# The last tile's output in a half and two quarters, its first LoRA half behind the mix of tile 14, and the gather index on VectorE

## The reference

```
x = x + einsum('bct,bcd->bdt', x, W0[cond])
base = einsum('bti,oi->bto', x, W) + b
lora = einsum('btr,bro->bto', einsum('bti,bir->btr', x, A[adapter]), B[adapter])
return x + base + lora * 2
```

## Time and profile before

| | |
|---|---|
| median of the runs (lowest, highest) | 85.22 us (85.20, 85.53) |
| the profiled execution | 85.35 us, of which its span is 83.6 us |
| busy: PE, DVE, ACT, POOL | 79.6, 59.3, 52.0, 35.0 us |
| granted clock of TensorE | full (1.0, the level of 2.4 GHz) in all slices |
| chain that ended last | PE 85%, DMA 6%, ACT's queue 3%, ACT 2%, issue 1%, DVE 1% |
| stores of 256 KB, of 128 KB (the last two) | 2.4 us, 1.7 us from issue to landing |

### The profile page before, as it was taken

How to read it: one execution, slowest core, us unless ns; L and a number is a source line. 1 busy time by engine, 2 the same in 40 slices (tenths; PEclk the granted TensorE clock), 3 DMA queues, 4 the chain that set the end, 5 groups by cost and what they waited for, 6 DMA issues and landing times.

```text
span 83.6 us, 1999 instructions
## 1 busy us (share of the span) xinstructions
PE 79.6 (95%) x521; PEld 71.8 (86%) x521; DVE 59.3 (71%) x154; ACT 52.0 (62%) x179; POOL 35.0 (42%) x75
## 2 busy tenths in 40 slices
PE   4999999999999999999999999999999999999970
PEld 2368688999899999999999999999999999999930
DVE  2048495885888787777878787888787777876540
ACT  1545757766566675958666666666685957669120
POOL 6128888844442617080715344342617080303000
PEclk9999999999999999999999999999999999999999
DMA  0999779899776768676586878676874734120333
GB/s 13 307 347 315 143 199 261 165 365 329 209 239 163 239 196 245 197 206 213 143 250 171 238 178 241 174 248 151 219 211 159 177 110 152 45 92 7 119 125 125
DMA packets 15997, 16.06 MB, mean 192 GB/s; under 512 B 10225, under 2 KB 10482, under 8 KB 15986
## 3 DMA queue, kind: packets, MB, share of 16 engines
q1 hardware_dynamic: 14016, 11.74, 47.4%
q0 software_dynamic: 1248, 4.06, 17.0%
q10 hardware_dynamic: 722, 0.14, 0.9%
HBM read 11.74 MB, written 4.19 MB: 191 GB/s over the span
## 4 chain that ended last, share of the span: by engine, by line
PE 85%; DMA 6%; ACTq 3%; ACT 2%; issue 1%; DVE 1%
PE z_ps L548 58%; PE z_ps L585 9%; DMA a_raw<-in_lora_a 6%; PE y_ps L596 4%; PE y_ps L600 4%; PE y_ps L598 4%; PE ht_ps L572 2%; ACTq L323 1%; PE z_ps L580 1%; PE ht_ps L626 1%; ACT L317 1%; PE y_last L608 1%; PE y_ps L608 1%; ACTq L313 1%; DVE y_sb L534 1%
## 5 line engine op out<-in xcount | busy, mean ns | idle before, releaser
L548 PE MATMUL z_ps<-wa,x_hi 128*128 128x288 f32 (+2 forms) x240 | 50.3, 301 | 0.0
L548 PEld LDWEIGHTS z_ps<-wa,x_hi 128*128 128x128 f32 x240 | 38.0, 188 | 1.8 <-issue 0.5
L548 PE MATMUL z_ps<-wa,x_lo 128*128 128x288 f32 (+2 forms) x120 | 35.5, 296 | 0.0
L548 PEld LDWEIGHTS z_ps<-wa,x_lo 128*128 128x128 f32 x120 | 22.6, 188 | 0.0
L291 POOL DMA_INDIRECT b_raw<-in_lora_b,b_index_slot x16 | 17.6, 1097 | 4.4 <-POOL b_index_slot L289 4.4
L300 POOL CAST m_hi<-m_raw 128x128 fp32r<-128x128 f32 x15 | 4.4, 293 | 31.5 <-ACT m_raw L337 31.5
L480 DVE TENSOR_TENSOR z_lo<-z_ps,z_hi 128x256 fp32r<-128x256 f32 x30 | 11.3, 420 | 6.4 <-ACT z_hi L381 6.4
L381 ACT CAST z_hi<-z_ps 128x256 fp32r<-128x256 f32 x30 | 9.7, 376 | 9.7 <-PE z_ps L585 9.6
L337 ACT COPY m_raw<-w_raw 32x32 f32 x64 | 13.8, 216 | 1.8 <-DVE w_raw L502 1.2
L439 DVE TENSOR_TENSOR x_lo<-x_raw,x_hi 128x512 fp32r<-128x512 f32 x14 | 9.7, 690 | 3.5 <-ACT x_hi L349 3.5
L460 DVE TENSOR_TENSOR b_lo<-b_raw,b_hi 128x512 fp32r<-128x512 f32 x15 | 10.4, 693 | 1.6 <-ACT b_hi L369 1.1
(11 more groups left out here) (51 smaller groups left out, 78.8 us busy)
## 6 DMA issues: line engine op xcount, KB each, us to landing
out<-y_sb SPq DMA_DIRECT2D x15, 256.0 KB, 2.4
x_raw<-in_xt SPq DMA_DIRECT2D x14, 256.0 KB, 2.9
a_raw<-in_lora_a SPq DMA_DIRECT2D x60, 32.0 KB
first_sb<-in_first SPq DMA_DIRECT2D x2, 384.0 KB, 4.0
first_sb<-in_first SPq DMA_DIRECT2D x3, 256.0 KB, 4.8
b_raw<-in_lora_b,b_index_slot POOLq DMA_INDIRECT x16, 4.0
bias_sb<-in_bias SPq DMA_DIRECT2D x1, 256.0 KB, 5.2
out<-y_sb SPq DMA_DIRECT2D x2, 128.0 KB, 1.7
```

The lines of the kernel that those rows point to most:

```text
L548: done = nc.tensor.matmul(target, (x_lo if lo_x else x_hi)[s][:, k, :], moving(lo_w), start=first and not lo_x and not lo_w, stop=last and ...
```

## The change

- GpSimd no longer makes `b_index`; VectorE does (`index_b`), behind its second `add_identity` and ahead of the first `rest_w`.
- TensorE's list for the last tiles: `transpose_h(14)` moves ahead of `mix(13)`, `lora(14)` behind that mix and ahead of chunks 2 and 3 of tile 15's half 0; `last_chunk(2, 1)` moves behind `mix(14)` and `lora(15, 0)`.
- Half 0 of tile 15 is mixed like other tiles, in three split matmuls of 256 columns (`mix_last_half`), half 1 in two fp32 matmuls of 128 columns (`mix_last_quarter`), the last one into the `ht_ps` bank. ScalarE rounds half 0 and copies half 1 in quarters; VectorE makes the rest of half 0; GpSimd splits M of tile 15 too.
- Bias adds and stores go by half, quarter, quarter; the last store is issued from ScalarE's queue.
- On ScalarE `round_h(15)` and `build_m(15)` move behind `round_z(14)`; on VectorE `mask_ht(14)` moves ahead of `rest_b(15)`, and `rest_h(15)` behind `rest_z(14)`.

```diff
+    PARTS = (slice(0, HALF), slice(HALF, HALF + P), slice(HALF + P, O))
...
+        def y_part(n):
+            return (y_ps[LAST % 2][:, 0:HALF], y_last[:, 0:P], ht_ps[:, 0:P])[n]
...
-            pool.wait_ge(ids_p_loaded, 16)
-            pool.tensor_copy(r_of_p[:, :], ids_p_sb[:, TILES:TILES + 1]).then_inc(r_ready, 1)
-            pool.wait_ge(r_ready, 1)
-            pool.tensor_scalar(b_index[:, :], ids_p_sb[:, 0:TILES], float(R), r_of_p[:, 0:1],
-                               ALU.mult, ALU.add).then_inc(b_index_ready, 1)
...
-            for u in range(LAST):
+            for u in range(TILES):
                 split_m(u)
...
-            build_m(LAST)
-            round_h(LAST)
             for half in range(2):
                 round_z(LAST - 1, half)
-            for half in range(2):
-                act.wait_ge(lora_done, 2 * LAST + half + 1)
-                act.copy(z_sb[:, cols(half)], z_of(LAST, half)).then_inc(z_copied, 1)
+            round_h(LAST)
+            build_m(LAST)
+            round_z(LAST, 0)
+            act.wait_ge(lora_done, 2 * LAST + 2)
+            for n in range(2):
+                act.copy(z_sb[:, n * P:(n + 1) * P], z_of(LAST, 1)[:, n * P:(n + 1) * P]).then_inc(z_copied, 1)
+            act.wait_ge(y_ready, LAST + len(PARTS))
+            act.dma_start(out_rows[LAST * P:(LAST + 1) * P, PARTS[-1]],
+                          y_sb[LAST % 2][:, PARTS[-1]]).then_inc(last_part_stored, 16)
...
+            add_identity(1)
+            index_b()
+            rest_w(0)
+            for k in range(1, KC - 1):
...
             rest_h(LAST - 1)
+            mask_ht(LAST - 1)
             rest_b(LAST)
-            mask_ht(LAST - 1)
             finish_y(LAST - 2)
-            rest_h(LAST)
             rest_z(LAST - 1, 0)
             rest_z(LAST - 1, 1)
+            rest_h(LAST)
             mask_ht(LAST)
             finish_y(LAST - 1)
+            rest_z(LAST, 0)
...
+            def mix_last_half():
+                pe.wait_ge(z_hi_ready, 2 * LAST + 1)
+                pe.wait_ge(m_ready, LAST + 1)
+                pe.wait_ge(y_ready, LAST - 1)
...
+            def mix_last_quarter(n):
+                pe.wait_ge(z_copied, n + 1)
...
-            mix_last(0)
-            mix_last(1)
+            mix_last_half()
+            mix_last_quarter(0)
+            mix_last_quarter(1)
```

More of the change, by code:

```diff
@@ L98, in lora_residual_program @@
         z_lo = [sb(f"z_lo{s}", [P, O], F32R) for s in range(2)]
-        z_sb = sb("z_sb", [P, O], F32)
+        z_sb = sb("z_sb", [P, HALF], F32)
         y_sb = [sb(f"y_sb{s}", [P, O], F32) for s in range(2)]
@@ L116, in lora_residual_program @@
         y_stored = [sem(f"y_stored{s}") for s in range(2)]
+        last_part_stored = sem("last_part_stored")
         zeros_ready = sem("zeros_ready")
@@ L250, in _ @@
             store_y(LAST - 1)
-            for half in range(2):
-                sp.wait_ge(y_ready, LAST + 1 + half)
-                sp.dma_start(out_rows[LAST * P:(LAST + 1) * P, cols(half)],
-                             y_sb[LAST % 2][:, cols(half)]).then_inc(y_stored[LAST % 2], 16)
+            for n, at in enumerate(PARTS[:-1]):
+                sp.wait_ge(y_ready, LAST + 1 + n)
+                sp.dma_start(out_rows[LAST * P:(LAST + 1) * P, at],
+                             y_sb[LAST % 2][:, at]).then_inc(y_stored[LAST % 2], 16)
             sp.wait_ge(y_stored[0], 16 * (TILES // 2))
             sp.wait_ge(y_stored[1], 16 * (TILES // 2 + 1))
+            sp.wait_ge(last_part_stored, 16)
         @block.gpsimd
@@ L488, in finish_y, with index_b @@
                                         ALU.add).then_inc(y_ready, 1)
+            def index_b():
+                dve.wait_ge(ids_p_loaded, 16)
+                nc.vector.tensor_copy(r_of_p[:, :], ids_p_sb[:, TILES:TILES + 1]).then_inc(r_ready, 1)
+                dve.wait_ge(r_ready, 1)
+                nc.vector.tensor_scalar(b_index[:, :], ids_p_sb[:, 0:TILES], float(R), r_of_p[:, 0:1],
+                                        ALU.mult, ALU.add).then_inc(b_index_ready, 1)
             dve.wait_ge(ident_ready, 1)
             add_identity(0)
-            for k in range(KC - 1):
+            add_identity(1)
+            index_b()
+            rest_w(0)
+            for k in range(1, KC - 1):
                 add_identity(k + 1)
@@ L522, in _ @@
             rest_h(LAST - 1)
+            mask_ht(LAST - 1)
             rest_b(LAST)
-            mask_ht(LAST - 1)
             finish_y(LAST - 2)
-            rest_h(LAST)
             rest_z(LAST - 1, 0)
             rest_z(LAST - 1, 1)
+            rest_h(LAST)
             mask_ht(LAST)
             finish_y(LAST - 1)
+            rest_z(LAST, 0)
             dve.wait_ge(y_stored[LAST % 2], 16 * (LAST // 2))
[L532 to L535, removed]
+            for n, at in enumerate(PARTS):
+                dve.wait_ge(y_computed, LAST + 1 + n)
+                nc.vector.tensor_tensor(y_sb[LAST % 2][:, at], y_part(n), bias_sb[:, at], ALU.add).then_inc(y_ready, 1)
         @block.tensor
@@ L601, in mix @@
                                  skip_group_check=True).then_inc(y_computed, 1)
[L603 to L609, removed]
+            def mix_last_half():
+                s = LAST % 2
+                pe.wait_ge(z_hi_ready, 2 * LAST + 1)
+                pe.wait_ge(m_ready, LAST + 1)
+                pe.wait_ge(y_ready, LAST - 1)
+                nc.tensor.matmul(y_part(0), m_hi[s][:, :], z_hi[s][:, cols(0)], start=True, stop=False,
+                                 skip_group_check=True)
+                nc.tensor.matmul(y_part(0), m_lo[s][:, :], z_hi[s][:, cols(0)], start=False, stop=False,
+                                 skip_group_check=True)
+                pe.wait_ge(z_ready, 2 * LAST + 1)
+                nc.tensor.matmul(y_part(0), m_hi[s][:, :], z_lo[s][:, cols(0)], start=False, stop=True,
                                  skip_group_check=True).then_inc(y_computed, 1)
+            def mix_last_quarter(n):
+                pe.wait_ge(z_copied, n + 1)
+                nc.tensor.matmul(y_part(1 + n), m_raw[LAST % 2][:, :], z_sb[:, n * P:(n + 1) * P], start=True,
+                                 stop=True, skip_group_check=True).then_inc(y_computed, 1)
             def first_chunk(k):
@@ L654, in _ @@
             last_chunk(1, 0)
+            transpose_h(LAST - 1)
             mix(LAST - 2)
-            transpose_h(LAST - 1)
+            lora(LAST - 1, 0)
+            lora(LAST - 1, 1)
             last_chunk(2, 0)
             last_chunk(3, 0).then_inc(main_done, 1)
-            lora(LAST - 1, 0)
-            lora(LAST - 1, 1)
             last_chunk(0, 1)
@@ L663, in _ @@
             transpose_h(LAST)
-            last_chunk(2, 1)
             mix(LAST - 1)
             lora(LAST, 0)
+            last_chunk(2, 1)
             last_chunk(3, 1)
             lora(LAST, 1)
-            mix_last(0)
-            mix_last(1)
+            mix_last_half()
+            mix_last_quarter(0)
+            mix_last_quarter(1)
 def kernel(**inputs):
```

## The result

The changed kernel takes 84.68 us (median of five, 84.62 to 84.87) against 85.40 for the kernel before on the same chip (85.20 to 85.53): ratio 0.9925, 95% interval 0.9902 to 0.9948. The forecast was 84.7 against 85.22. The profiled execution has a span of 83.0 us instead of 83.6.

What follows compares the result with a forecast made beforehand. TensorE, busy 79.6 of 83.6 us, bounds the kernel; only stalls, start and end can shorten it. Gains 0.06 + 0.14 + 0 + 0.22 + 0.13 = 0.55 us take the median from 85.22 to 84.7, range 84.35 to 85.3.

Steps and rivals of the forecast that it cites:

- Index earlier: At the start, `b_index` made on VectorE stands 1.3 us earlier, gathers 0 to 2 go out about 1.2 us sooner.
- The stall before tile 0's LoRA: TensorE's loads idle 0.26 us before tile 0's LoRA matmuls, waiting for gather 0; a stall of some 0.2 goes.
- The cap: Tile 2's first matmul needs `z_lo` of tile 0, so the earlier gather gains 0.06 us there, not 0.2.
- Tile 2's 0.16: Late gather 2 stretches tile 2's four LoRA matmuls from 0.48 to 0.64 us; an earlier gather gains 0.14.
- The forecast's 0.20: Gain of the start together, 0.06 at tile 2's start plus 0.14 at its LoRA; bounds 0 and 0.42 us.
- TensorE's order: Near the end, a 0.11 us stall before tile 15's transpose replaces one of 0.11 at `mix(14)`: net 0.
- M of tile 15: Split M is there at 79.3, TensorE wants it at 79.42: cost 0; at worst 0.3 us.
- Last mix: Tile 15's mix by half and quarters ends the last add near 81.17 instead of 81.39: 0.22 us gained.
- The store: Last store, 64 KB from ScalarE, lands in 1.6 us against 1.7 for 128 KB: 0.13 gained with the free issue.
- the tight waits: Rival: four waits near the end with 0.06 to 0.1 slack eat the gain; price 0.25 to 0.4, 85.0; chance 0.25.
- The exclusion at the start: Rival: gather 0's issue shuts VectorE out, or gather 2 lands no sooner; price 0.2 to 0.5 us, chance 0.15.
- The slow store: Rival: ScalarE's last store lands late, price 0 to 0.8 us, decided from 2.15 us to landing; chance 0.1.

Runs made afterwards that it cites:

- the second series: The changed kernel run again beside the kernel before and the changed kernel with the index back on GpSimd: 84.86 us, ratio 0.9947 to before.
- e5_z_first: Changed kernel with ScalarE's rounding of z of tile 0 ahead of its block copies for M: 85.21 us, ratio 1.0023 to the kernel before.
- b_again: The kernel before, unchanged, run again for a second profile; no time given, 65.52 us from adapter copy to mark.
- e8_late_index: Changed kernel with the index, still on VectorE, moved behind the third `rest_w`: 85.60 us, ratio 1.0044 to the kernel before.
- e9_tail_again: Changed kernel with the index back on GpSimd, run again beside the changed kernel: 85.01 us, ratio 0.9968 to the kernel before.
- the end alone: Changed kernel with the index back on GpSimd: 84.91 us, ratio 0.9943 to the kernel before; 85.01 us when run again.
- e7_order: Changed kernel with tile 15 mixed as before, in two fp32 matmuls of 256 columns, and two SyncE stores: 85.13 us, ratio 0.9972 to before.
- e3_sp_store: Changed kernel with the last quarter's store issued by SyncE instead of ScalarE: 85.25 us, ratio 0.9983 to the kernel before.
- e1_index: The kernel before with only the index moved to VectorE: 85.09 us, ratio 0.9964 to the kernel before.
- e4_half_whole: Changed kernel with half 1 of tile 15 whole: one copy, matmul, add and store; 85.04 us, ratio 0.9993 to the kernel before.
- b_third: The kernel before, unchanged, run a third time for its profile: 87.57 us.

## Why the prediction was right, and where its terms were not

The mechanism at the end was right; the terms of the start were right in their sum and not in their parts. That the number was met to 0.02 us is luck in part. In the profiled pair an earlier landing of 0.22, which no term had, and 0.10 more than forecast up to the last add stand in for the store (0.07 lost, 0.13 gained by the forecast) and for tile 2's start (0.07 lost, 0.06 gained by the forecast). And the second series has the changed kernel at 84.86, 0.36 under the kernel before (85.22) and not 0.55.

- *Index earlier: right.* Forecast 1.3 us, measured 1.46; the gather 1.42 earlier instead of 1.2. I took 0.2 for each VectorE instruction; they took 0.15 and 0.23.
- *The stall before tile 0's LoRA: mis-sized, and misread.* I took the idle 0.26 for the gather and let it go. 0.16 remain in every profile with an early gather (0.17 in two), so only 0.10 were the gather's in the first profile. The row puts the idle time down to "issue", and I overrode it by the landing time, which explained only a part.
- *The cap: right, and tighter.* `z_lo` of tile 0 sets tile 2's start, as the new wait at 14.97 shows; `e5_z_first` removed that wait. Forecast gain 0.06, measured 0 or a loss of 0.07: between adapter copy and tile 2 it is 5.98 before and 5.98 to 6.05 after. From `z_lo`'s end to the load I allowed 0.05; it takes 0.11, in the changed kernel (14.86 to 14.97) and before (15.01 to 15.12). So `z_lo` was already there no sooner than tile 2's load needed it.
- *Tile 2's 0.16: the step that failed.* I took 0.14 for certain. It shows in one of the five profiles in which gather 2 was issued late: `b_again` has 0.47, and `e8_late_index`, later still, 0.49. The mechanism was there: the earlier issue brought gather 2 in at 15.5 instead of 19.4, and the rival that it would be no sooner in full queues was wrong. But without the first execution's last microsecond TensorE does not feel it.
- *What the index is worth instead.* Gather 0 must land within about 3.1 us of the adapter copy (TensorE reaches tile 0's LoRA 3.26 behind the copy, and a load starts 0.15 behind the landing), and both scatter: by 0.05 to 0.1 it is late in two profiles with the old index, by 0.42 in one, by 1.35 in one, and in time in one; in none of the eight profiles with the index on VectorE ahead of the first `rest_w`. `e8_late_index` gives the size: 0.75 us late cost 0.75; in `e9_tail_again` 0.42 cost 0.3 to 0.4. The 0.05 to 0.1 cost nothing that shows, as `z_lo` holds tile 2 up as long. The medians go the same way: 0.9964 for the index alone, and 0.15 us between the changed kernel and the end alone in one series (84.86, 85.01). The forecast's 0.20 was thus met, if it was, by another mechanism. That this difference is real rests on intervals that overlap, and the mechanism on five profiles of the old index; the ratios of the two parts are larger than their marks (0.49 us for the end alone, where mark to span's end gives 0.26), which their intervals allow.
- *The earlier adapter landing, 0.22 in the profiled pair,* is scatter: 8.68 to 9.28 over all profiles, on average 8.91 with the index on GpSimd (five) and 9.03 on VectorE (the eight with early gathers), so not earlier by the change. The forecast had no term for it.
- *TensorE's order: right.* One stall replaces the other: forecast 0.11 for 0.11, measured 0.07 for 0.11; `e7_order` gives 0.04 in all.
- *M of tile 15: right.* Forecast 0.12 to spare, measured 0.14. The register load behind the rounding of h was in the open, 0.34 of idle ScalarE, as foreseen.
- *Last mix: right, larger.* Forecast 0.22, measured 0.29 from the last LoRA matmul's end to the last add's end (79.71 to 81.39 before, 79.36 to 80.75 now). The adds of VectorE follow at 0.22 where I put 0.27 between the quarters, and half 0's add starts at once.
- *The store: wrong size.* Forecast 0.13 gained. 64 KB land in 1.8 us, not 1.6; from the last add to the span's end it is 2.30 against 2.23, and so in every pair of profiles (2.28 to 2.31 with the quarter on ScalarE, 2.23 to 2.24 with the half on SyncE): 0.06 to 0.07 lost. But ScalarE's queue was needed: three SyncE issues would have cost 0.26 more (`e3_sp_store`).

Of the rivals, the tight waits did not bite in any profile. The exclusion at the start bit almost one way: GpSimd waits for VectorE (0.57 for 0.19, and 0.91 for 0.28). VectorE's instructions kept their 0.69 beside the first gather's 1.42, and only one that begins just ahead of an issue takes 0.06 more: 0.75 for 0.69 in the changed kernel, `e1_index`, `e4_half_whole` and `e5_z_first`. The strict reading of the rule in the Trainium skill (page "SBUF — State Buffer", section "Who interferes with whom"), by which VectorE would be shut out for the whole of a gather's issue, was not met by any row here. The section does not say it of a gather's issue either: it infers that making descriptors needs the write interface, where a `tensor_tensor` takes only the read one; the 0.06 is what the rows have beyond that. The slow store came in part: 1.8 us, short of the 2.15 that would have decided.

## What to carry to other kernels

A long piece in one profile is a property of that execution until a second profile of the same kernel shows it; ask for two before it enters a sum as a certain gain. Read in each of them, too, how long before its use the operand lands: that tells a near miss from a safe margin. An operand that arrives just in time on average is late in some executions, and there it may cost more than its lateness. At the end of a kernel, work back from the last store by part: halves of the last copy, matmul and add overlap, until one engine's adds stand back to back, and the stores' issues want more than one queue.

## What the runs showed of the hardware

- Idle time of TensorE's loads of 1.5 us, up to 13.3, was followed by 3.4 us at a granted clock of 0.5, from 15.3 on; with the lateness itself it cost 2.7 us up to the mark (`b_third`). Idle times of 0.58 and 0.91 in the same place were not followed by it.
- Gather 2 took 4.1 to 5.3 us to land when it was issued at 10.25 to 10.65, and 5.9 to 7.6 when it was issued at 11.54 to 12.57.
- The last store landed in 1.8 us from ScalarE and in 1.7 from SyncE, and 64 KB were no faster than 128 KB.
- The landing of the four small adapter transfers scatters by 0.6 us between executions of nearly the same program, and moves everything behind it by as much.
- A GpSimd instruction that reads SBUF took 0.28 begun in a gap of VectorE and 0.91 beside VectorE's additions of two SBUF operands; such a VectorE instruction took 0.75 instead of 0.69 when a gather's issue began 0.02 behind its start.
